# A NF4 feed-forward and S4 layer on one core: other orders in the opening, each unit's low half behind the next scaled whole, and early down units at other tiles

## The reference, cut to what matters

```python
x = L0_attn_u                                  # 4 x 512 x 512: 2048 tokens of width 512
xn = _layernorm(x, axis=-1)
x = x + _L0_attn_ref(xn, ...) + _L0_ffn_ref(xn, ...)
# _L0_ffn_ref: M = 1792, codes q in 0..15, a scale per 64 weights
Wg, Wu = dequant_nf4(gate_q, ...), dequant_nf4(up_q, ...)    # 1792 x 512
Wd = dequant_nf4(down_q, ...)                                # 512 x 1792
h = silu(xn @ Wg.T) * (xn @ Wu.T)
return h @ Wd.T
# _L0_attn_ref: a kernel K of 512 values (S4, Cauchy sums, inverse FFT),
# then a causal convolution of each row of xn with K, plus D * xn
```

## Time and profile before

| what | value |
|---|---|
| median of 3 runs | 471.67 us (471.19 to 472.29) |
| profiled execution, its own time | 471.57 us |
| its span | 469.7 us, so 1.87 us lie around it |
| PE busy | 440.0 us (94%) |
| DVE busy | 396.7 us (84%) |
| ACT busy | 280.8 us (60%) |
| POOL busy | 209.1 us (45%) |

### The profile page before, as it was taken

How to read it: one execution, slowest core, us unless ns; L and a number is a source line. 1 busy time by engine, 2 the same in 40 slices (tenths; PEclk the granted TensorE clock), 3 DMA queues, 4 the chain that set the end, 5 groups by cost and what they waited for, 6 DMA issues and landing times.

```text
span 469.7 us, 7270 instructions
## 1 busy us (share of the span) xinstructions
PE 440.0 (94%) x2556; PEld 250.5 (53%) x2556; DVE 396.7 (84%) x629; ACT 280.8 (60%) x472; POOL 209.1 (45%) x180
## 2 busy tenths in 40 slices
PE   0789799999898699999999999999999999999997
PEld 0554344444343244444444444456544688888886
DVE  5966877988997979898897777969999799999993
ACT  7748737576787595687776767956232543545340
POOL 2672597364858685466655655957400000000000
PEclk9999999999999799999999999999999999999999
DMA  8461547111322454242512243347694021001101
GB/s 290 118 232 69 99 93 164 43 50 64 126 89 68 166 200 138 66 158 68 181 45 67 56 104 90 89 138 248 192 342 157 1 91 45 25 22 46 46 30 62
DMA packets 34168, 51.41 MB, mean 109 GB/s; under 512 B 13076, under 2 KB 14164, under 8 KB 33364
## 3 DMA queue, kind: packets, MB, share of 16 engines
q1 hardware_dynamic: 34132, 50.95, 35.1%
HBM read 38.03 MB, written 10.81 MB: 104 GB/s over the span
## 4 chain that ended last, share of the span: by engine, by line
PE 66%; DVE 12%; POOL 9%; issue 7%; ACT 4%; DMA 1%; SPq 0%; POOLq 0%; DVEq 0%; ACTq 0%
PE bank L2290 29%; PE bank L2417 21%; PE bank L2367 8%; PE bank L2357 6%; POOL work L885 3%; PE bank L2134 3%; ACT work L977 2%; POOL w L898 2%; DVE work L1350 1%; DVE h L1424 1%; DMA h<-in_x 1%; DVE work L1354 1%; DVE h L1539 1%; DVE h L1440 1%; POOL wd L898 1%
## 5 line engine op out<-in xcount | busy, mean ns | idle before, releaser
L977 ACT ACTIVATE work<-work 128x512 f32<-128x512 f32 (+1 forms) x234 | 130.2, 623 | 17.4 <-POOL work L885 11.4
L885 POOL TENSOR_SCALAR work<-work 128x512 f32<-128x512 int32 x39 | 85.1, 2182 | 69.5 <-DVE work L1350 56.6
L2290 PE MATMUL bank<-h 128*128 128x512 f16 x360 | 81.6, 379 | 0.5 <-DVE h L1411 0.4
L2134 PE MATMUL bank<-xT,w 128*128 128x512 f16 (+1 forms) x312 | 67.2, 374 | 4.4 <-DVE xT L1591 2.5
L2290 PEld LDWEIGHTS bank<-h 128*128 128x128 f16 x360 | 34.9, 98 | 43.8 <-issue 1.2
L2417 PE MATMUL bank<-wd,work 128*128 128x256 f16 x504 | 56.2, 273 | 0.0
L2290 PE MATMUL bank<-xT,w 128*128 128x512 f16 x240 | 55.4, 379 | 0.0
L2417 PEld LDWEIGHTS bank<-wd,work 128*128 128x128 f16 (+1 forms) x504 | 49.3, 98 | 6.0
L2134 PEld LDWEIGHTS bank<-xT,w 128*128 128x128 f16 x312 | 31.4, 101 | 37.5 <-DVE w L1364 3.1
L898 POOL TENSOR_SCALAR w<-work,sc 128x512 f16<-128x512 f32 x21 | 40.3, 1921 | 21.9 <-DVE work L1354 21.3
L1290 ACT ACTIVATE work<-h 128x896 f16<-128x896 f32 x30 | 27.9, 942 | 28.5 <-DVE h L2042 18.3
(11 more groups left out here) (196 smaller groups left out, 661.9 us busy)
## 6 DMA issues: line engine op xcount, KB each, us to landing
moved<-h SPq DMA_DIRECT2D x6, 1024.0 KB, 5.1
h<-moved SPq DMA_DIRECT2D x4, 1536.0 KB, 15.3
h<-in_x SPq DMA_DIRECT2D x8, 512.0 KB, 4.6
xT<-in_x SPq DMA_DIRECT2D x16, 256.0 KB, 3.6
out<-xT SPq DMA_DIRECT2D x15, 256.0 KB, 2.1
work<-in_q_gate SPq DMA_DIRECT2D x14, 256.0 KB, 2.8
work<-in_q_up SPq DMA_DIRECT2D x14, 256.0 KB, 3.1
work<-in_am_gate SPq DMA_DIRECT2D x28, 128.0 KB, 3.0
```

The lines of the kernel that those rows point to most:

```text
L885: pool.tensor_scalar(chain_room(u, "r"), qs[:, u % 2, :], RIGHT_FROM, RIGHT_FROM, ALU.max, ALU.subtract).then_inc(first_done, 1)
L977: nc.scalar.activation(room, qs[:, u % 2, :] if j == 0 else room, KNEE, scale=scale, bias=bias, alpha=below).then_inc(knee_done, 1)
L2134: mm = nc.tensor.matmul(out_b, weights(k)[:, unit, wl, f, :], xT[:, TPC * c + first:TPC * c + last, xl, f, :], start=(i == 0), stop=(i == ...
L2290: mm = nc.tensor.matmul(out_b, weight(wl, f), token(xl, f), start=(n == 0 and i in (1, 5)), stop=(n == 5), skip_group_check=i not in (1, 5))
```

## The change

It alters orders, and moves no arithmetic but one: the reciprocal roots of chunk 3 are now made on DVE by the twelve steps that the other chunks use, and POOL's seventeen are gone. In the opening ACT, DVE, POOL, SP and PE get other orders: DVE splits tiles 0 to 3 and units 0 and 1 ahead of the statistics of tiles 5 to 7; units 7 and 8 are scaled much earlier; the token sums of chunks 0 and 1 (`token_whole(1, ...)`) move from window 3 into the opening, with other waits. In every later unit the low half of unit u-1 comes behind the scaled whole of u (items 3, 4, 2), and the sums with an up unit come right behind its scaling. Early down units are made in windows 7, 8, 9, 11 and not in 5, 6, 9, 12. Left out of the diff are the declarations of `rs_next`, the body of POOL's `rstd`, and SP's loop, which no longer issues `absmax_of(8)`.

```diff
@@ -119,7 +119,7 @@
-EARLY_IN = (5, 6, 9, 12)
+EARLY_IN = (7, 8, 9, 11)
...
@@ -689,6 +688,7 @@
     codes_of(8)
+    absmax_of(8)
     sp.dma_start(lstep, log_step.to_broadcast([P, 1])).then_inc(step_ld, 16)
...
@@ -739,51 +740,10 @@
-    def rstd(c):
...
-        if c < 3:
-            pool.wait_ge(rs_step, RSTD * (c + 1))
-        else:
-            pool.wait_ge(rs_next, RSTD_NEXT)
+        pool.wait_ge(rs_step, RSTD * (c + 1))
@@ -911,22 +871,21 @@
         norm(t)
     first_pass(2)
     first_pass(3)
+    first_pass(4)
     for t in range(TPC, 2 * TPC):
         norm(t)
-    first_pass(4)
     first_pass(5)
     for i in range(14):
         v_step(i)
     first_pass(6)
     for t in range(2 * TPC, 3 * TPC):
         norm(t)
-    rstd(3)
+    first_pass(7)
     for t in range(3 * TPC, NT):
         norm(t)
-    first_pass(7)
+    first_pass(8)
     for i in range(EXP_STEPS):
         exp_step(i)
-    first_pass(8)
     for u in POOL_HALVES:
         if u + 2 < UNITS:
             first_pass(u + 2)
@@ -1141,59 +1100,60 @@
     chain(1, 0, 5)
     norm(0)
     chain(1, 5, 6)
-    chain(2, 0, 1)
     x_hi(0)
     weight_hi(0)
     x_hi(1)
-    chain(2, 1, 2)
+    chain(2, 0, 1)
     x_hi(2)
     x_hi(3)
+    chain(2, 1, 2)
     weight_hi(1)
     chain(2, 2, 6)
     chain(3, 0, 2)
     weight_hi(2)
-    chain(3, 2, 6)
+    chain(3, 2, 4)
     x_hi(4)
+    chain(3, 4, 6)
+    silu(0)
+    chain(4, 0, 1)
+    weight_hi(3)
     x_hi(5)
-    weight_hi(3)
+    x_hi(6)
     act.wait_ge(b_mm, 1)
     nc.scalar.activation(yv[:, 0:2], bank[3][:, 0:2], ACT.Copy).then_inc(b_cp, 1)
-    x_hi(6)
     x_hi(7)
-    chain(4, 0, 3)
-    silu(0)
-    chain(4, 3, 6)
-    chain(5, 0, 3)
+    chain(4, 1, 6)
     h_hi(0)
     silu(1)
     weight_hi(4)
-    chain(5, 3, 6)
+    chain(5, 0, 6)
     h_hi(1)
+    silu(2)
     x_hi(8)
     weight_hi(5)
     x_hi(9)
     x_hi(10)
     x_hi(11)
-    silu(2)
+    silu(3)
     chain(6, 0, 6)
-    silu(3)
     silu(4)
     h_hi(4)
+    silu(5)
+    chain(7, 0, 6)
     x_hi(12)
     x_hi(13)
     x_hi(14)
     x_hi(15)
-    chain(7, 0, 6)
-    silu(5)
     silu(6)
+    chain(8, 0, 6)
     silu(7)
     silu(8)
     silu(9)
-    items(ACT_AT[7], ACT_AT[7] + 3)
+    weight_hi(6)
+    gate_copy(6)
     token_hi(0, 0)
     token_hi(0, 2)
     silu(10)
-    items(ACT_AT[7] + 3, ACT_AT[8])
     token_hi(0, 1)
     token_hi(0, 3)
     items(ACT_AT[8], ACT_AT[8] + 1)
@@ -1334,9 +1294,8 @@
             else:
                 dve.wait_ge(clamp_done, CLAMPS_AT[u + 1])
                 dve.wait_ge(dq_done, dq_after(u, LEFT))
-            if u >= 2:
-                dve.wait_ge(wlo_done, u - 1 if u < 4 or u in CHAINED else u)
+            if u >= 3:
+                dve.wait_ge(wlo_done, u - 2)
             past = u - 1
             if u in CHAINED:
                 past = u - 3 if u - 3 >= CHAINED[0] - 1 else None
@@ -1368,14 +1327,13 @@
         for p in range(first, last):
             u, i = item_of(DVE_AT, p)
             if u in CHAINED:
-                i = (3, 2, 4)[i]
+                i = (3, 4, 2)[i]
             if i != 2:
                 step(u, i if i < 2 else i - 1)
             elif u > 0:
                 weight_lo(u - 1)
-                before = SEQ[u - 1]
-                if before < GU and before % 2 == 1 and before // 2 in BLOCKED:
-                    up_sums(before // 2, u - 1)
+            if i == 4 and SEQ[u] < GU and SEQ[u] % 2 == 1:
+                up_sums(SEQ[u] // 2, u)
     def up_sums(k, u):
@@ -1418,8 +1376,10 @@
         c, f = (ROLE_E, ROLE_B)[i % 2][s], 2 * (i // 2)
         if s == 0 and f == 0:
             dve.wait_ge(xt_ld[c - 2], 16 * TPC)
+        elif s == 1 and i == 2:
+            dve.wait_ge(xp_done, NT - POOL_NORMS)
         elif s == 1 and i == 0:
-            dve.wait_ge(xlo_done, NT)
+            dve.wait_ge(xt_ld[1], 16 * TPC)
         hi, lo = (xT[:, TPC * c:TPC * c + TPC, l, f:f + 2, :] for l in (HI, LO))
         v.tensor_tensor(x_sums[s][i].rearrange("p (f t m) -> p t f m", f=2, t=TPC), hi, lo,
                         ALU.add).then_inc(xb_done[s], 1)
@@ -1622,115 +1582,134 @@
     stats(4)
     scales(6)
     step(0, SCALED)
+    step(1, WHOLE)
+    scales(7)
+    scales(8)
+    x_lo(0)
+    weight_lo(0)
+    x_lo(1)
+    step(1, SCALED)
+    x_lo(2)
+    x_lo(3)
+    weight_lo(1)
     stats(5)
     stats(6)
-    scales(7)
     stats(7)
-    scales(8)
     moments(4, 8)
-    step(1, WHOLE)
     rstd(1, 0)
     rstd(1, 1)
     rstd(1, 2)
-    x_lo(0)
+    scales(9)
     rstd(1, 3)
-    weight_lo(0)
     rstd(1, 4)
-    x_lo(1)
     rstd(1, 5)
-    step(1, SCALED)
+    step(2, WHOLE)
     rstd(1, 6)
     rstd(1, 7)
-    x_lo(2)
     rstd(1, 8)
-    x_lo(3)
+    step(2, SCALED)
     rstd(1, 9)
     rstd(1, 10)
-    weight_lo(1)
     rstd(1, 11)
-    scales(9)
-    step(2, WHOLE)
-    scales(10)
-    step(2, SCALED)
-    scales(11)
     weight_lo(2)
     stats(8)
+    x_lo(4)
+    scales(10)
     step(3, WHOLE)
+    scales(11)
+    step(3, SCALED)
+    h_mul(0)
     scales(12)
-    step(3, SCALED)
-    x_lo(4)
+    weight_lo(3)
     x_lo(5)
-    weight_lo(3)
+    x_lo(6)
     stats(9)
-    x_lo(6)
     x_lo(7)
     stats(10)
-    h_mul(0)
     stats(11)
     moments(8, 12)
     rstd(2, 0)
     rstd(2, 1)
     rstd(2, 2)
-    h_lo(0)
+    step(4, WHOLE)
     rstd(2, 3)
-    step(4, WHOLE)
     rstd(2, 4)
     rstd(2, 5)
     step(4, SCALED)
     rstd(2, 6)
     rstd(2, 7)
     rstd(2, 8)
-    h_mul(1)
+    h_lo(0)
     rstd(2, 9)
     rstd(2, 10)
     rstd(2, 11)
+    h_mul(1)
     weight_lo(4)
+    step(5, WHOLE)
+    step(5, SCALED)
     h_lo(1)
-    step(5, WHOLE)
+    stats(12)
     x_lo(8)
-    step(5, SCALED)
-    stats(12)
+    stats(13)
     weight_lo(5)
     x_lo(9)
-    stats(13)
     x_lo(10)
+    x_lo(11)
+    h_mul(2)
     stats(14)
-    x_lo(11)
     stats(15)
     moments(12, 16)
-    h_mul(2)
+    rstd(3, 0)
+    rstd(3, 1)
+    rstd(3, 2)
     h_mul(3)
+    rstd(3, 3)
+    rstd(3, 4)
+    rstd(3, 5)
     step(6, WHOLE)
+    rstd(3, 6)
+    rstd(3, 7)
+    rstd(3, 8)
     step(6, SCALED)
+    rstd(3, 9)
+    rstd(3, 10)
+    rstd(3, 11)
+    token_whole(0, 1)
     h_mul(4)
-    token_whole(0, 1)
+    token_whole(0, 3)
     h_lo(4)
-    token_whole(0, 3)
+    h_mul(5)
+    step(7, WHOLE)
+    step(7, SCALED)
     for t in range(12, 16):
         x_lo(t)
-    h_mul(5)
     h_mul(6)
-    items(DVE_AT[7], DVE_AT[7] + 1)
+    step(8, WHOLE)
+    step(8, SCALED)
+    token_whole(1, 2)
+    token_whole(1, 3)
     h_mul(7)
-    h_mul(8)
     token_whole(0, 0)
     token_whole(0, 2)
     token_sum(0, 0)
+    h_mul(8)
     token_sum(0, 1)
+    token_sum(0, 2)
+    token_whole(1, 0)
     h_mul(9)
-    items(DVE_AT[7] + 1, DVE_AT[8])
-    token_sum(0, 2)
     token_sum(0, 3)
+    weight_lo(6)
     token_lo(0, 0)
     token_lo(0, 2)
+    token_whole(1, 1)
     h_mul(10)
     token_lo(0, 1)
+    weight_lo(7)
+    up_sums(BLOCKED[0], 7)
     token_lo(0, 3)
-    items(DVE_AT[8], DVE_AT[8] + 2)
     other_sums(BLOCKED[0])
     h_mul(11)
     block_lo(BLOCKED[0], 0)
-    items(DVE_AT[8] + 2, DVE_AT[9])
     block_lo(BLOCKED[0], 1)
     def mixed_window(k):
@@ -1740,17 +1719,13 @@
         n = NCH * k
         if k == 3:
-            token_whole(1, 0)
-            token_whole(1, 1)
             h_mul(n)
             h_lo(n)
             join(0, k, 0)
-            part(0, 4)
-            token_whole(1, 2)
+            part(0, 5)
             join(0, k, 1)
             h_mul(n + 3)
-            token_whole(1, 3)
-            part(4, 6)
+            part(5, 6)
         else:
             part(0, 2)
             token_sum(1, 1)
@@ -2193,11 +2168,9 @@
     products(1, (0,))
     turn(5)
     turn(6)
+    turn(7)
     pe.wait_ge(b_cp, 1)
-    pe.wait_ge(wlo_done, PLACE[3] + 1)
-    product(1, 1, 0, 2)
-    turn(7)
-    product(1, 1, 2, TPC).then_inc(up_done, 1)
+    products(1, (1,))
     for n in range(2, len(OPENING)):
         _, c = ORDER[n]
```

More of the change, by code:

```diff
@@ L492, in ffn_conv_kernel @@
         rs_step = sem("rs_step")
-        rs_next = sem("rs_next")
         xn_done = sem("xn_done")
@@ L560, in ffn_conv_kernel @@
         TURNED = 8
-        RSTD, RSTD_NEXT = 12, 17
+        RSTD = 12
         SUMMED = (1,)
@@ L703, in _ @@
                 codes_of(place + 1)
-                absmax_of(place)
+                if place > 8:
+                    absmax_of(place)
                 if place == LINE_AT:
@@ L740, in _ @@
                                pattern=[[-1, P]], channel_multiplier=1).then_inc(id_done, 1)
-            def rstd(c):
[L744 to L776, removed]
-                pool.wait_ge(rs_next, at + 16)
-                pool.tensor_tensor(bias, bias, scale, ALU.mult).then_inc(rs_next, 1)
```

## The result

The changed kernel takes 459.5 us (median of 4 runs, 459.0 to 460.59) where the kernel before takes 471.75 in the same comparison: a ratio of 0.9744 [0.9723, 0.9764], 12.2 us less. The forecast was 459.7, within 456 to 465. The profiled execution took 460.59, with a span of 458.8. In it DVE waits 1.14 us for a DMA of the input tokens at 7.62, and from there on every step starts 0.76 us later than in the profiled execution of before (PE's first transposes at 12.99 against 12.23).

The account below looks back on a forecast made before the run. The kernel was taken as bound by PE's work plus DVE's lateness at six places. Gains of 3.5 - 0.9 + 2.2 + 5.1 + 2.0 = 11.9 us cut the span from 469.7 to 457.8, 459.7 with 1.87 around it; range 456 to 465.

Parts of the forecast that it names:

- unit 5 with no wait: Opening: PE's 2.59 us wait for unit 5 goes, its low half at 47.0 against PE at 47.2; 5.2 ahead in all.
- `weight_lo(9)` at 1.07 for 0.9: Window 3: the low half, now behind both `block_lo`, ends at 111.9 against PE at 111.0; 0.9 lost, 2.6 ahead.
- the clock's 2.0: Behind the 5.40 us join wait: 2.0 us more gained since PE's clock no longer falls to 0.50.
- two counts, 147.1 and 145.5: End of tile 5's join, PE asking at 146.5: a sum gave 147.1 (0.6 wait), a step by step walk 145.5.
- rival 1: DVE stays the bound in windows 3 to 5, PE waits 2 to 4 us at the join: 463.1, worst 466; chance 0.20.
- the windows' 7.3 (2.2 + 5.1): Windows from `weight_lo(9)` to tile 5's join: 2.2 from waits of 1.74 and 0.45, 5.1 from the 5.40 wait.
- PE transposes tile 4 at 26.1: Opening: chunk 1's roots come at 24.9, POOL's first norm takes 1.0, so the early start is mostly eaten there.
- Cost 0: Windows 7 and 8 get a third down unit, 2.1 us on DVE; 1.1 late is covered by joins 2.1 early.
- if it starts to wait in windows 7 to 9: Sign that the forecast is wrong: PE starting to wait in windows 7 to 9.
- The wait of 1.4 for chunk 3's DMA transposes: Opening, chunk 3: transposes land at 72, PE is there at 70.6; one new wait of 1.4, leaving 3.7 ahead.
- the 0.35 that was to stay: Window 13: PE's wait of 0.35 us was to remain.
- Slower: Rival 4: DVE overruns windows 7 to 9 and 11 with three units; at 3.3 each, 472.9; chance 0.03.

Follow-up runs that it names:

- f2: Changed kernel with 18 extra matmuls of 256 columns, results unused, in PE's wait ahead of the transposes of tile 4: 459.37 us, 0.9712 of the kernel before.
- e5: Changed kernel's opening alone, with the old order inside a unit and down units back in windows 5, 6, 9, 12: 465.42 us, 0.9871 of the kernel before.
- f3: Changed kernel with two DVE moves in its windows: chunk 0's `h_mul` one stage sooner where three units, chunk 1's join ahead of slot 5: 459.33 us.
- g1: Changed kernel with f3's two moves in window 8 only, `weight_lo(9)` ahead of `h_mul(14)`, and ACT's copy of `yv` right behind `weight_hi(2)`: 456.78 us, 0.9671.
- e1: Changed kernel with the early down units back in windows 5, 6, 9, 12: 461.58 us, 0.9772 of the kernel before.
- e4: Kernel before with only the new order inside a unit: 471.13 us, 0.9977 of the kernel before.
- e6: Kernel before with the new order inside a unit and down units in windows 7, 8, 9, 11, old opening: 470.17 us, 0.9951.
- e2: Changed kernel with the old order inside a unit, sums of an up unit back behind its low half: 462.33 us, 0.9791 of the kernel before.
- e3: Kernel before with only the down units moved to windows 7, 8, 9, 11: 467.91 us, 0.9918 of the kernel before.
- f0: The changed kernel itself, run again as reference for f2 and f3: 459.76 us, 0.9727 of the kernel before.
- g2: g1 with f2's extra matmuls: 457.06 us, 0.9677 of the kernel before.

## Why the prediction was right, and where its steps were not

How far PE is ahead of before at each checkpoint, the 0.76 of the later start added to the measured figure:

| checkpoint | forecast | before | after | measured |
|---|---|---|---|---|
| first product | 2.5 | 19.16 | 17.80 | 2.1 |
| tile 2, first product | 2.4 | 47.03 | 46.50 | 1.3 |
| chunk 3's first product | 3.7 | 75.69 | 72.40 | 4.1 |
| product 5 of tile 3 | 3.5 | 97.70 | 94.42 | 4.0 |
| behind `weight_lo(9)` | 2.6 | 114.54 | 112.49 | 2.8 |
| product 4 of tile 5 | 9.9 | 156.69 | 146.17 | 11.3 |
| product 4 of tile 6 | 11.9 | 176.83 | 164.30 | 13.3 |
| product 4 of tile 8 | 11.9 | 213.09 | 203.24 | 10.6 |
| convolution | 11.9 | 308.29 | 297.33 | 11.7 |
| span | 11.9 | 469.7 | 458.8 | 11.7 |

*What holds.* The places where the time came from were as forecast: the wait at the first product, unit 5 with no wait, product 5 of tile 3, `weight_lo(9)` at 1.07 for 0.9, the join of tile 5 (no wait, where 0.3 was taken), the clock's 2.0. DVE no longer waits for POOL's high half in windows 4 and 5. DVE's walk to the join:

```profile
142.86 1.10 DVE L1323 SCALAR_TENSOR_TENSOR w<-work,sc,w 128x512 f16<-128x512 f32 x1
...
145.13 0.68 DVE L1412 TENSOR_TENSOR h<-bank,h 128x512 f32<-128x512 f32 x1
```

It ends at 145.8 and PE asks at 146.17; without the 0.76 it ends at 145.0. Of the two counts, 147.1 and 145.5, the step by step walk was the right one. The cover is 0.4 us, so rival 1 was near.

*What was mis-sized: the windows' 7.3 (2.2 + 5.1).* It measured 8.5 (11.3 - 2.8). From 114.54 to 156.69 PE's timeline of before has waits of 1.74, 0.45 and 5.40, 7.6 in all, and about 0.16 more at each of them that the bracket does not count: twelve matmuls started at 148.54 are over 2.59 later, at 151.13, and 156.69 - 5.40 is 151.29. That is 0.5. Two groups of before also ran longer, by 0.2 each:

```profile
117.15 2.98 PE L2290 MATMUL bank<-h 128*128 128x512 f16 x12
...
135.44 5.50 PE L2290 MATMUL bank<-h 128*128 128x512 f16 x24 [0.45 <-DVE h L1411]
```

where the changed kernel shows 2.75 and 5.34. These make 8.5.

*What failed: ACT's copy, unit 3's low half and the clock, in the opening.* "PE transposes tile 4 at 26.1" was priced as a wait only. Stretches of the changed kernel; the columns are the length, PE, PEld, DVE, ACT, POOL, then the granted clock, the DMA share and GB/s:

```profile
26.00:27.00 1.00, 0.00 (x0) 0.00 (x0) 0.68 (x2) 1.00 (x3) 0.83 (x3) 0.73 0.12 47
27.00:28.00 1.00, 0.97 (x5) 0.91 (x6) 1.00 (x2) 0.43 (x1) 1.00 (x1) 0.50 0.66 193
```

PE stood for 2.45 us, and came back at 0.50. The transposes took 0.9 up to the next group where f2's took 0.5, and the twelve matmuls 3.55 for 2.6: 1.3 us on PE. Part of that is hidden. In e5, with the same opening and the clock at 1.00, PE waits 1.45 for ACT's copy of `yv`, and its product starts 20.4 us behind its first transposes (33.31 - 12.87); here it is 20.6 (33.54 - 12.99), in f2 19.8. So beside e5 the clock costs 0.1, beside f2 up to 0.8. What PE waits for is the copy, which I hadn't in this stretch, and directly in front of it unit 3's low half, which ended at 33.24, or 32.5 without the 0.76, where I had 31.5. The low half is 1.0 of the shortfall and the copy 0.3. Some of the 1.0 can itself come from the slow transposes, for which ACT waits 0.76 us here and 0.29 in f2. So tile 2 starts 1.3 ahead and not 2.4.

*What failed: "Cost 0" for the later down units.* Window 8 has two waits, 2.0 together, and windows 7 and 8 cost 2.7 in all. DVE's timeline there:

```profile
188.10 0.87 DVE L1798 TENSOR_TENSOR wd<-wd 128x256 f32<-128x256 f32 x2
188.89 0.74 DVE L1438 SCALAR_TENSOR_TENSOR work<-bank,sc,h 128x512 f32<-128x512 f32 x1
...
190.22 1.09 DVE L1309 SCALAR_TENSOR_TENSOR work<-work 128x512 f32<-128x512 f32 x1
191.24 1.74 DVE L1798 RECIPROCAL wd<-wd 128x256 f32<-128x256 f32 x1
...
196.01 0.68 DVE L1412 TENSOR_TENSOR bank<-bank,h 128x512 f32<-128x512 f32 x1
```

and ACT's:

```profile
189.73 0.58 ACT L1029 ACTIVATE bank<-bank 128x512 f32<-128x512 f32 x1 [3.42 <-DVE work L1438]
```

I compared DVE's sum with the window's length, 19.2 in 18.1, and set the 1.1 against joins that were early. The sum was right (DVE is busy for 19.0 us from 180.19 to 200.65, and the window took 20.5). What counted was the place in the list: `h_mul` stands behind scaling, sums and an S4 stage, ACT's copy waits 3.42 for it and PE 0.95 for the copy. The second join stands behind a reciprocal of 1.74 and two more steps. f3 and g1 show it: the same DVE work with two steps moved leaves 0.75 and 0.7 of the 2.0 in this window. By the prediction's own sign ("if it starts to wait in windows 7 to 9") this part of its mechanism was wrong, though the time stayed in the range.

*What failed in the other direction.* The wait of 1.4 for chunk 3's DMA transposes didn't come. PE got there at 72.40, 1.0 later than I had (71.6 without the 0.76, against 70.6), and the last transpose, which SP issued at 68.6, landed some 3.2 later, about 71.8 (an estimate, 71.0 without the 0.76), 1.0 sooner than my 72. So there 4.1 stands for 3.7. And from product 4 of tile 12 (288.76, 278.78) to the convolution before took 19.53 us and the changed kernel 18.55: the 0.35 that was to stay went, with 0.6 more.

*The sum.* 11.9 was forecast for the span and 10.9 measured, 11.7 without the late start. It comes out by errors that offset: +1.4 up to the join of tile 5, -2.7 in windows 7 and 8, +1.1 behind them. The medians are 12.2 apart because the profiled execution of the changed kernel lay 1.1 above its median, that of before 0.2 under it. So the total is right to 0.2 us by luck as well, and the single parts to 1 or 2.

*POOL.* Its high half went from 1574 to 1820 ns at the median, and from 3361 to 2755 at most. The trace of the changed kernel:

```profile
L858 POOL TENSOR_SCALAR w<-work,sc x21: 1573/1820/2755, 79.9 to 267.4; 128x512 f16<-128x512 f32 x21
```

DVE waited 5.4 and 3.2 us for this step in all of before, and 1.9 and 1.4 now. No wait of PE names POOL's high half, so the dearer median is hidden. It goes with the order of the items, not with the opening: 1821, 1822 and 1824 ns in e1, e4 and e6, which have the new order, and 1573, 1740 and 1737 in e5, e2 and e3, which have the old one. A longest one of 3360 or 3361 stands in all three with the old order, and e4 has one of 5544. The Trainium skill (SBUF — State Buffer, Who interferes with whom) calls the shared port pair an exclusive lock. That fits a median that moves with what DVE does at the same time, but no run here separates the lock from other causes, and a median beside a maximum, which the prediction called agreement, doesn't show it either.

*The rivals.* None of the five came. The first names a length of wait above which the clock falls; the last section shows that the length doesn't decide it. Slower: window 8 did start to wait, but at 2.0 in all and not 3.0 in each window.

## What to carry to other kernels

A window's sum of work says whether an engine keeps up, and not whether one step is in time: walk the list to each step that another engine waits for, and look for the next one behind it. An order that delays one step to bring another forward is worth something only with a lead to pay it from, so try such edits together as well as alone (here the order brought nothing clear of noise alone, and 0.0099 beside the opening). Ask of a slower run also where in its trace it fell behind: e6 did so ahead of the part that had been changed. When a wait can't be removed, ask what it does to the clock, and then whether the time is hidden anyway.

## What the runs showed of the hardware

Waits of 2 to 3 us had two outcomes for the granted clock, even at one and the same place. Before and e6 have the same order of instructions on every engine up to 82 us. PE stands for 2.59 us in both for unit 5's low half. In before the clock is at 1.00 from 50 to 59 us; in e6 it has fallen before PE is back at 52.73:

```profile
52.00:53.00 1.00, 0.27 (x1) 0.13 (x2) 1.00 (x2) 1.00 (x3) 0.00 (x0) 0.59 1.12 212
53.00:54.00 1.00, 1.00 (x4) 0.32 (x3) 1.00 (x3) 1.00 (x3) 0.00 (x0) 0.50 0.13 25
```

Ahead of the transposes of tile 4 the clock fell in the changed kernel (2.45), where it was at 0.50 when PE came back. It came back at 1.00 and fell 0.9 and 1.3 us later in f0 (2.53) and g1 (2.88), and it stayed at 1.00 in e5 (2.75 ahead of 27.25), where twelve matmuls took 2.6. Elsewhere it fell in e4 behind 2.08, 1 us after PE was back, and in e5 at 285 behind a wait of 2.05 with one of 0.36 shortly before. It stayed up in before behind 2.54, in e1 behind 2.15 and in e6 behind 2.30. Stretches of e4; its product starts at 97.13:

```profile
97.00:98.00 1.00, 0.87 (x4) 0.41 (x5) 1.00 (x3) 1.00 (x3) 1.00 (x1) 1.00 0.00 0
98.00:99.00 1.00, 1.00 (x4) 0.40 (x3) 1.00 (x2) 0.30 (x1) 1.00 (x1) 0.60 0.65 176
```

So in this range neither the length of a wait nor its place in the program decided. What does wasn't tried. An execution can therefore lose or keep 1 to 2 us at such a wait with no change in the kernel, which is as much as the smaller effects above. The price on PE was 1.3 (changed kernel), 1.4 (e6), 1.7 (f0), 2.0 (before, behind 5.40) and 2.5 us (e5, behind 5.40), and where a later step covered it only part of that reached the end (f2) or nothing that the medians show (g2). Behind the 5.40 us waits of before and e5 the clock was at 0.50 in both.
